# A four-layer graph network on one core: the attention layer rewritten tile by tile, layer norms moved to ScalarE

## The reference

```python
Xq = (H @ W_lin.T).reshape(bt, n, h, dh);  Xv = (H @ W_val.T).reshape(bt, n, h, dh)
e = einsum('behd,hd->beh', leaky_relu(Xq[:, src] + Xq[:, dst], 0.2), a)
e = e + log(A0[src, dst] + 1e-8)[None, :, None]
attn = softmax of e over the edges that share a src
Y = segment_sum(attn[..., None] * Xv[:, dst], src);  return Y.reshape(bt, n, d) @ W_out.T
```

## Time and profile before

| what | us |
|---|---|
| median of three runs | 1168.74 |
| profiled execution | 1168.33 |
| its span (first to last instruction) | 1166.5 |
| TensorE busy | 975.3 (84%) |
| VectorE busy | 743.4 (64%) |
| ScalarE busy | 535.5 (46%) |
| GpSimd busy | 158.7 (14%) |

### The profile page before, as it was taken

The page is one execution under the profiler, slowest core; times in us unless marked ns, Lnnn a source line. Parts: engine busy times, 40 slices in busy tenths (PEclk is TensorE's granted clock), DMA queues, the critical chain, the costliest instruction groups (busy, mean ns, idle before and its releaser), DMA issues.

```text
span 1166.5 us, 15574 instructions
## 1 busy us (share of the span) xinstructions
PE 975.3 (84%) x4413; PEld 666.3 (57%) x4413; DVE 743.4 (64%) x2552; ACT 535.5 (46%) x1387; POOL 158.7 (14%) x390
## 2 busy tenths in 40 slices
PE   4788867878667775995996799989999999999995
PEld 3555545555555654753774788868644456654443
DVE  4567676647678873697666688853454455564576
ACT  1455535537245652332343122223596565555556
POOL 0122222203222220000000000000001111120054
PEclk9699967869565555997997899989999999999998
DMA  9000000000000000000000000000000000000013
GB/s 262 10 1 1 1 1 2 1 1 2 1 1 1 1 1 1 1 1 0 0 0 1 0 0 0 0 1 1 1 1 0 1 1 0 1 1 0 1 36 108
DMA packets 14317, 12.86 MB, mean 11 GB/s; under 512 B 896, under 2 KB 11056, under 8 KB 14256
## 3 DMA queue, kind: packets, MB, share of 16 engines
q1 hardware_dynamic: 14018, 11.98, 3.7%
q10 hardware_dynamic: 238, 0.16, 0.0%
HBM read 7.89 MB, written 4.19 MB: 10 GB/s over the span
## 4 chain that ended last, share of the span: by engine, by line
PE 63%; DVE 24%; issue 5%; ACT 5%; POOL 1%; DVEq 1%; DMA 0%; SPq 0%; POOLq 0%; ACTq 0%
PE bank L844 14%; PE bank L868 8%; PE bank L791 3%; PE bank L776 3%; PE bank L735 3%; PE bank L741 2%; PE bank L749 2%; PE bank L470 2%; PE bank L576 2%; PE bank L811 1%; PE bank L463 1%; PE bank L830 1%; PE bank L817 1%; PE bank L822 1%; DVE hid_t L1942 1%
## 5 line engine op out<-in xcount | busy, mean ns | idle before, releaser
L1268 ACT ACTIVATE hid_t<-bank,gate_b 128x512 f32<-128x512 f32 (+1 forms) x252 | 150.8, 631 | 67.9 <-PE bank L868 66.8
L868 PE MATMUL bank<-ms,w_t 128*128 128x512 f32 (+1 forms) x288 | 112.8, 535 | 6.8 <-DVE ms L1960 6.8
L844 PE MATMUL bank<-hid_t,w_t 128*128 128x336 f32 (+1 forms) x296 | 106.5, 507 | 1.2 <-DVE x L1964 1.2
L1361 POOL COPY hid_t<-feat_t 128x1008 f32<-128x1008 f32 (+1 forms) x12 | 27.8, 2320 | 581.1 <-DVE feat_t L1956 581.1
L844 PE MATMUL bank<-feat_t,w_t 128*128 128x512 f32 x208 | 93.1, 603 | 0.0
L868 PEld LDWEIGHTS bank<-ms,w_t 128*128 128x128 f32 x288 | 54.5, 192 | 56.5 <-issue 34.2
L844 PEld LDWEIGHTS bank<-hid_t,w_t 128*128 128x128 f32 x296 | 56.2, 191 | 46.1 <-issue 26.3
L844 PEld LDWEIGHTS bank<-feat_t,w_t 128*128 128x128 f32 x208 | 39.2, 189 | 51.0 <-issue 46.7
L1275 ACT ACTIVATE hid_t<-hid_t 128x512 f32<-128x512 f32 (+1 forms) x72 | 41.8, 581 | 52.2 <-DVE hid_t L1942 27.6
L1115 ACT ACTIVATE hs<-bank,con 128x1 f32<-128x1 f32 x62 | 16.2, 261 | 102.4 <-PE bank L577 102.4
L1942 DVE TENSOR_TENSOR hid_t<-hid_t 128x512 f32<-128x512 f32 (+1 forms) x36 | 42.2, 1173 | 17.0 <-ACT hid_t L1268 16.9
(11 more groups left out here) (434 smaller groups left out, 2292.8 us busy)
## 6 DMA issues: line engine op xcount, KB each, us to landing
out<-x SPq DMA_DIRECT2D x16, 256.0 KB, 2.6
con<-in_constants SPq DMA_DIRECT2D x1, 449.0 KB, 3.3
hid_t<-in_L_gnn_W SPq DMA_DIRECT2D x2, 128.0 KB, 3.7
e_int<-in_L_gnn_src ACTq DMA_DIRECT2D x1, 128.0 KB
l_w<-in_L_gnn_W SPq DMA_DIRECT2D x2, 64.0 KB
wg<-in_L_gnn_Wg SPq DMA_DIRECT2D x2, 64.0 KB
adj_n<-in_adj SPq DMA_DIRECT2D x1, 64.0 KB, 3.7
hid_t<-in_L_gnn_W_lin SPq DMA_DIRECT2D x1, 64.0 KB, 3.4
```

The source lines that it names most:

```text
L844: return mm(bank[4 * u + BANK_OF[g]][:, 0:w], w_t[:, WB_IH + 4 * (it.p - 1) + g, :], lstm_x(n), start=True, stop=(it.k == 0))
L868: mm(bank[4 * u + BANK_OF[g]][:, 0:w], w_t[:, WB_HH + 4 * (it.p - 1) + g, :], lstm_h_of(it.chain)[:, 0:w], start=False, stop=True).then_in ...
L1268: f(dst[:, 0:w], bank[4 * u + BANK_OF[g]][:, 0:w], ACT.Tanh if g == G_G else ACT.Sigmoid, bias=gate_b[:, 4 * (it.p - 1) + g:4 * (it.p - 1) ...
L1361: pool.tensor_copy(turned[:, g * nb * P:g * nb * P + nb * nw * p].rearrange("q (k a n) -> q k a n", k=p, a=nb), feat_t[:, g * nb:(g + 1) * ...
```

## The change

Nothing changes outside layers 1 to 3 but where the final norm keeps its statistics (they move from `xs[0]` to `perm`). In the changed kernel all hardware loops of these layers are written out.

**Norms.** In layers 1 and 2 VectorE no longer writes the normalised x. It adds into x in place, takes statistics (eight batches together in layer 1, four in layer 2) and computes scale and shift; ScalarE writes x in place. ScalarE's write of a tile stands two turns behind.

**Logits.** Each tile of x is transposed on TensorE, evicted, and used as the held operand against W_lin and W_val side by side (256 columns). The two halves of the result are evicted apart: `z_lin` and `z_val` (in `feat_t`, kept for all 16 tiles). Edge columns are gathered from `z_lin`. The logits are a product that holds a 128-column window of `head_strip` (zeros, with the head vector's 4 columns in one place) and streams the activations; the window slides by 4 rows a batch, and 32 batches add up in one bank. The log of the edge weight is brought to a row by two products with ones.

**Softmax** by halves of 32 batches: the first between tiles 9 to 14 of the logits loop, the second between tiles 0 to 6 of the values loop.

**Values.** The dst rows are gathered from `z_val` by holding `dst_st` and streaming 512 columns. Banks 4 and 5 are now single for the sum by src and for W_out.

**Layer 3** waits for each tile of x by itself.

```diff
+            def ln_written(count, t):
+                act.wait_ge(s["ln_scale"], count)
+                for b in range(TB):
+                    d = f(x[:, t * TB + b, :], x[:, t * TB + b, :], ACT.Identity,
+                          scale=ln_rs[:, t, b:b + 1], bias=ln_shift[:, t, b:b + 1])
+                d.then_inc(s["x_ready"], 1)
```

TensorE's order and products:

```diff
+            def layer2():
+                l2_turn(0)
+                for t in range(TILES):
+                    l2_project(t)
+                    if t + 1 < TILES:
+                        l2_turn(t + 1)
+                    if t == 0:
+                        gcn_floor()
+                    if t == 1:
+                        gcn_bias()
+                    if t:
+                        l2_logits(t - 1)
+                    l2_gather(t)
+                soft_turn(0)
+                l2_values(0)
+                l2_logits(TILES - 1)
+                for t in range(TILES):
+                    if t + 1 < TILES:
+                        l2_values(t + 1)
+                    if t:
+                        l2_out(t - 1)
+                    if t == 6:
+                        soft_turn(1)
+                    l2_scatter(t)
+                l2_out(TILES - 1)
...
+            def l2_turn(t):
+                    d = tr(bank[t % 2][:, b * P:(b + 1) * P], x[:, t * TB + b, :], ident)
...
+            def l2_project(t):
+                        d = mm(bank[2 + k][:, b * E:(b + 1) * E], xs[t % 2][:, 2 * k + b, :], w_t[:, WB_LIN:WB_LIN + 2, :],
+                               start=True, stop=True)
...
+            def l2_gather(t):
+                for k, name in enumerate(("l2_z_act", "l2_z_dve")):
+                    pe.wait_ge(s[name], t + 1)
+                    if t:
+                        pe.wait_ge(s["l2_act"], 2 * t + k - 1)
+                    for b in range(2):
+                        d = mm(bank[4 + k][:, b * E:(b + 1) * E], z_lin[t % 2][:, 2 * k + b, :], sum_st[:, :], start=True, stop=True)
...
+            def l2_logits(t):
+                        r = HEADS * (TB * (t % PAIRS) + 2 * k + b)
+                        d = mm(bank[6 + half][:, 0:E], head_strip[:, P - HEADS - r:2 * P - HEADS - r], rhs[:, b * E:(b + 1) * E],
+                               start=(r == 0), stop=(r == P - HEADS))
...
+            def l2_values(t):
+                    mm(bank[2 * (t % 2) + c][:, :], dst_st[:, c * P:(c + 1) * P], z_val[:, t * TB:(t + 1) * TB, :],
+                       start=True, stop=True).then_inc(s["l2v_val"], 1)
...
+            def l2_scatter(t):
+                pe.wait_ge(s["l2v_w"], 2 * (t + 1))
+                if t:
+                    pe.wait_ge(s["l2v_y_sb"], t)
+                        d = mm(bank[4][:, b * P:(b + 1) * P], w[c][:, b, :], src_s[:, c, :], start=(c == 0), stop=(c == EC - 1))
...
+            def l2_out(t):
+                pe.wait_ge(s["l2v_y_sb"], t + 1)
+                if t:
+                    pe.wait_ge(s["l2v_added"], t)
+                    d = mm(bank[5][:, b * P:(b + 1) * P], ms[t % 2][:, b, :], w_t[:, WB_OUT, :], start=True, stop=True)
```

ScalarE's order (`l2_turned` evicts the four transposes as 512 columns, `l2_kept` copies two times 256 columns out of bank 2, `l2_slope` and `l2_y_kept` are 512 columns each):

```diff
+            def layer2():
+                l2_turned(0)
+                for t in range(TILES):
+                    l2_kept(t)
+                    if t + 1 < TILES:
+                        l2_turned(t + 1)
+                    for k in range(2):
+                        l2_slope(t, k)
+                    if t < 4:
+                        l1_written(TILES - 4 + t)
+                    if t == 1:
+                        l1_root(PAIRS - 1)
+                    if t == 10:
+                        soft_exp(0)
+                for t in range(TILES):
+                    if t == 2:
+                        table_for(ACT.Sqrt)
+                    if t > 1:
+                        l2_root(t - 2)
+                    l2_y_kept(t)
+                    if t == 1:
+                        soft_exp(1)
+                    if t > 1:
+                        l2_written(t - 2)
```

VectorE's order (`l2_kept` copies two times 256 columns out of bank 3, `l2_weighted` is two products of 512 columns; the first half's softmax stands at t 9 to 14, the second half's logits, two maximum scans and difference at t 0, its other steps one a tile at t 1 to 6):

```diff
+            def layer2():
+                for t in range(TILES):
+                    l2_kept(t)
+                    if t == 0:
+                        floor_and_row()
+                        l1_stats(PAIRS - 1)
+                    if t == 1:
+                        gcn_bias()
+                    for k in range(2):
+                        l2_leaky(t, k)
+                    if t == 1:
+                        l1_scaled(PAIRS - 1)
...
+                soft_columns(0)
+                l2_weighted(0)
+                for t in range(TILES):
+                    if t + 1 < TILES:
+                        l2_weighted(t + 1)
+                    if t > 1:
+                        l2_scaled(t - 2)
+                    if t:
+                        l2_added(t - 1)
...
+                    if t:
+                        l2_stats(t - 1)
```

Layer 3 on TensorE:

```diff
             def layer3_gcn():
+                        pe.wait_ge(s["x_ready"], CREDIT + 2 * TILES + 2 * j + u + 1)
-                pe.wait_ge(s["x_ready"], CREDIT + 64)
```

More of the change, by code:

```diff
@@ L441, in edges @@
                 tr(py[0][0:1, 0:P], sc[:, 8:9], ident).then_inc(s["edge_adj"], 1)
-            def ahead(turns, early, work):
-                early(0)
-                with pe.Fori(0, turns - 1) as j:
-                    work(j, lambda: early(j + 1))
-                work(turns - 1, lambda: None)
             def ahead_written_out(turns, early, work):
@@ new lines, in gcn_floor, with gcn_bias @@
+            def gcn_floor():
+                pe.wait_ge(s["l1_added"], CREDIT + TILES)
+                mm(bank[6][:, 0:P], bg0[:, :], rowsum_t[:, :], start=True, stop=True).then_inc(s["gcn_floor"], 1)
+                for c in range(EC):
+                    d = mm(bank[7][:, c * P:(c + 1) * P], ones[:, :], diag_log[:, c, :], start=True, stop=True)
+                d.then_inc(s["log_row"], 1)
+            def gcn_bias():
+                pe.wait_ge(s["gcn_floor_sb"], 1)
+                pe.wait_ge(s["log_row_sb"], 1)
+                mm(bank[7][:, E:E + P], floor[:, :], wg1[:, :], start=True, stop=True).then_inc(s["gcn_floor"], 1)
@@ new lines, in layer1 @@
+                fetched(0)
+                fetched(1)
+                for j in range(PAIRS):
+                    for t in (2 * j, 2 * j + 1):
+                        act.wait_ge(s["l1_hid"], t + 1)
+                        f(ht[t % 2][:, :, :], ph[t % 2][:, :], ACT.Relu, bias=v_cols[:, VR_L1B1:VR_L1B1 + 1]).then_inc(s["l1_hid_sb"], 1)
+                    if j > 1:
+                        l1_written(2 * j - 4)
+                    if j + 1 < PAIRS:
+                        fetched(2 * j + 2)
+                        fetched(2 * j + 3)
+                    if j > 1:
+                        l1_written(2 * j - 3)
+                    if j:
+                        l1_root(j - 1)
@@ L1419, in norm_apply, with ln_added @@
-            def norm_apply(u, nb, first, tile):
-                dve.wait_ge(s["ln_std"], tile + 1)
-                link(dve.reciprocal(rs[:, u, 0:nb], rs[:, u, 0:nb]))
-                for b in range(nb):
-                    t = ts(x[:, bass.ds(first + b, 1), :], ys[u][:, b:b + 1, :], mv[:, u, b, 0:1], rs[:, u, b:b + 1],
-                           ALU.subtract, ALU.mult)
-                t.then_inc(s["x_ready"], 1)
-            def norm_scale(u, nb, tile):
-                dve.wait_ge(s["ln_std"], tile + 1)
-                link(dve.reciprocal(rs[:, u, 0:nb], rs[:, u, 0:nb]))
-                stt(shift[:, u, 0:nb], mv[:, u, 0:nb, 0], -1.0, rs[:, u, 0:nb], ALU.mult, ALU.mult).then_inc(s["ln_scale"], 1)
+            def ln_added(t, src, name):
+                tt(x[:, t * TB:(t + 1) * TB, :], x[:, t * TB:(t + 1) * TB, :], src[:, :].rearrange("p (a b) -> p a b", a=TB), ALU.add)\
+                    .then_inc(s[name], 1)
@@ L1517, in edges @@
                 dve.wait_ge(s["edge_adj"], 2)
[L1518 removed]
+                copy(rowsum_t[:, :], py[0][0:1, 0:P])
             def l0_stats(n):
@@ new lines, in l1_stats, with l1_scaled, head_rows @@
+            def l1_stats(j):
+                dve.wait_ge(s["l1_added"], CREDIT + 2 * j + 2)
+                ln_stats(2 * j, 2)
+            def l1_scaled(j):
+                ln_scaled(TILES + j + 1, 2 * j, 2)
+            def head_rows():
+                dve.wait_ge(s["log_done"], 1)
+                link(dve.memset(head_strip, 0.0))
+                link(copy(head_strip[:, P - HEADS:P], head_a[:, :]))
+                for c in range(EC):
+                    link(ts(diag_log[:, c, :], ident, log_a[:, c:c + 1], None, ALU.mult))
@@ new lines, in l2_kept, with l2_leaky @@
+            def l2_kept(t):
+                dve.wait_ge(s["l2_z"], 2 * t + 2)
+                z = bank[3][:, :].rearrange("p (b k d) -> p b k d", b=2, k=2)
+                copy(z_lin[t % 2][:, 2:4, :], z[:, :, 0, :])
+                copy(z_val[:, t * TB + 2:t * TB + 4, :], z[:, :, 1, :]).then_inc(s["l2_z_dve"], 1)
+            def l2_leaky(t, k):
+                dve.wait_ge(s["l2_slope"], 2 * t + k + 1)
```

(2 more changed lines are left out.)

507 lines of the change are left out of this document (234 added, 273 removed).

## The result

The changed kernel takes 1086.8 us (median of four runs, 1086.33 to 1087.05) against 1168.75: a ratio of 0.9298, 95% interval 0.9282 to 0.9314. A second measurement of the changed kernel gave 1088.06 us, so 0.2 us is less than what separates two medians of it.

What follows compares the result with a forecast made beforehand. TensorE was taken as the bound (63% of the last chain), with idle holes and low-clock starts. Gains of 72.2 plus 2.4 us, 74.6, off 1168.33 gave 1093.7; 2 us for missed waits made 1096, range 1087 to 1114.

Steps and rivals of the forecast that it cites:

- Holes and order: Layers 1 to 3: hole between layers 9.8 to 2.6 us, softmax's 19.05 us to 5.8, layer 3 saves 2.4.
- the smaller values turn: Values: turn falls from 7.19 to 4.64 us since norm write, two evictions and smaller tiles' fixed parts leave.
- the price of the values turn: Values: TensorE sets the turn at 4.64 us a tile, against 3.9 us of work on VectorE.
- The margins: Allowances for stalls in logits and values, and 2 us for 0.1 us waits missed in 40 turns.
- the sum of tile 7 ends about 1 us late: Values: TensorE leads by a turn and catches VectorE, slowed by the second softmax half; about 1 us.
- the way to the first sum: Between logits and values: four transposes, two values products and the last logits, 5.8 us, replace softmax's 19.05 us hole.
- the hole: Between layers 1 and 2: TensorE's wait shrinks to 2.6 us, ScalarE's eviction standing behind a root.
- Layer 1: Layer 1: norm writes leaving VectorE, 2 x 1.11 us a turn, bring turns from 7.96 to 7.3 us.
- Rival 4: Layer 1: ScalarE becomes the last engine, turns of 7.96 us again, +5, so 1101 us; chance 0.10.
- Rival 1: Values: single banks 4 and 5 tie the turn to VectorE, 5.6 us a turn, 1115 us; chance 0.12.
- Rival 2: Logits and values: tiles run one after another, +3.8 and +2.6 us a tile, 1199 us; chance 0.03.
- rival 3: Logits: transposes don't keep the clock up, 16 tiles cost 5.64 us more each, 1186 us; chance 0.01.

Runs made afterwards that it cites:

- u_wait_l2: Changed kernel, but attention's first transposes wait until all of layer 1's norms are written (last roots and writes moved ahead); 1097.05 us.
- u_softmax_one: Changed kernel, but the softmax of both halves runs in one piece between the logits and the values; 1100.77 us.
- u_wait_l3: Changed kernel, but layer 3's first products wait for all of layer 2's norms (last roots and writes moved ahead); 1094.17 us.
- u_norm_l2: Changed kernel, but VectorE writes the normalised x of layer 2 again, four batches a tile; 1093.30 us.
- u_norm_l1: Changed kernel, but VectorE writes the normalised x of layer 1 again, two tiles a turn; 1087.17 us.
- out_twice: Changed kernel with the four W_out products of each values tile issued twice, same result; 1100.53 us.
- half_heads: Changed kernel with half of the head products left out of the logits; 1072.81 us.
- fill_turns: u_wait_l2 with its pause filled by 64 transposes whose results nobody uses; 1096.62 us.
- fill_products: u_wait_l2 with its pause filled by 32 products (64 records) whose results nobody uses; 1097.66 us.

## Where the prediction was right, and why it was 9 us too high

**Holes and order: right.** The projection waits for the eviction behind the root, W_out waits for its eviction twice at the end (0.69 each, priced at 0.8), tile 0 and tile 1 of the logits cost 5.05 and 5.85 us (4.6 and 6.3 predicted), layer 3's first turn is free of the low clock. u_wait_l2, u_softmax_one and u_wait_l3 put single parts back and cost about what those parts were said to bring. By the middle these parts are worth 11.5, 15.8 and 7.1 us, each alone (they need not add up); the smaller values turn, about 4.4 against 7.19 in sixteen turns, is the largest, some 45 us, by the two traces and not by an undoing. The prediction gave it to work that leaves VectorE (the norm write, the evictions). u_norm_l2 puts the norm write back and loses 6.8 us in all; the rows above show that the products by W_val, 2.15 us a turn on TensorE, had to leave as well. The prediction's sum of TensorE's products has them gone, its reason does not name them. No run puts them back.

**The failed step: the price of the values turn.** "TensorE: 1.80 (two of 512) + 0.95 (W_out) + 1.89 (by src) = 4.64 us a tile." Measured 1.72 + 0.89 + 1.78 = 4.39. The mechanism was right here and the size off: these are start-to-start readings of the loops of before, and they hold something of those loops. Before, the sum by src came straight behind VectorE's weighting, so its held operand could not be loaded ahead; in the changed kernel that load starts 0.11 us before the product (660.27 and 660.38, above):

```profile
703.75 1.86 PEld L791 LDWEIGHTS bank<-src_s,ht 128*128 128x128 f32 x16 [0.29 <-DVE ht L1904]
```

There the product starts at 703.75 too and the group takes 1.89 us; with the load ahead it takes 1.78. The products of 512 columns are the same case in smaller: in the earlier trace rows load and product start within 0.02 us of each other (577.16, 577.18), in the changed kernel's values 0.11 apart, and they take 1.80 and 1.72. That these 0.1 us are real and not a fault of reading is seen in layer 1 of the changed kernel, whose second products still wait for the relu:

```profile
476.62 1.86 PEld L715 LDWEIGHTS bank<-l_w,ht 128*128 128x128 f32 x16 [0.75 <-ACT ht L1233]
```

The turn from there is 1.88 + 1.79 + 1.72 + 1.80 = 7.19 us; at 1.72 for products of 512 columns and 1.78 for those of 128 it would be 7.00. So the prices of before were right for groups whose load doesn't run ahead, and together 0.25 us a turn too high where TensorE leads by a turn, which the prediction itself had said of the values. The fourteen turns from 620.57 to 682.36 took 61.8 us against 65.0: 3.2 of the 4.15 us.

**The margins: hardly used.** I added 1 us for stalls in the logits, 1 in the values and 2 us for waits that a walk misses. In the logits TensorE is busy 89.56 us of 89.59; one turn, with the exponential's table load on ScalarE, took 5.91 us instead of 5.62 (587.24 to 593.15), so 0.3 of the first came. In the values the lead over VectorE, one turn, takes up the whole second softmax; "the sum of tile 7 ends about 1 us late" didn't happen. The margins (3.7 unused) and the turn's price (3.2) are 6.9 of the 9.4 us between the sum for the profiled execution (1093.7 and 2) and its time (1086.33); the rest is 0.8 in layer 1, 0.6 in the rest of the logits, 0.6 on the way to the first sum (two transposes too many, and again products of 512 columns at 1.80), 0.4 in the hole, 0.3 in the stage ahead, and crumbs of both signs.

**Layer 1: right number, wrong cause.** 7.3 forecast, 7.19 measured (469.43 to 476.63, and the same through to 519.78). I gave the gain to 2 x 1.11 us that left VectorE; u_norm_l1 put them back and nothing changed. VectorE's turn is 7.08 us with them, not 8.1: two operations on 512 columns back to back take 1.28 us, not 2 x 0.69, and the statistics of eight with their means and variances 2.43 (500.90 to 503.33), not 2.75, so I had also over-priced VectorE. So the right number owes nothing to the moved writes: with them or without, the turn is TensorE's 7.19 us. That it came out right is luck as far as the cause goes. The wait that I named in the earlier trace rows, a relu behind a root behind a variance, is gone in both forms; that it was the cause by itself is likely, not shown. Rival 4 (ScalarE as layer 1's last engine) did not come: the turn is 7.19, and the relu costs TensorE the 0.2 us above, no more.

**The other rivals.** Rival 1 (the single banks tie the values to VectorE) needed turns of 5.6; VectorE has 0.50 us to spare in a turn. u_norm_l2 shows the mechanism real and near: with 1.11 us more on VectorE, turns are 4.56 and the two before tile 6 lose 3.8. Rival 2 (tiles one after another) is refuted by out_twice and half_heads; rival 3 by fill_turns.

**The range.** Its low end stood 9 us under the forecast, and only 5 of them had a reason (table loads and statistics). It held no case "all my high readings and margins are nothing", though this was worth 7 us.

## What to carry to other kernels

Take a price from a turn in which the engine stands as it will stand in the new kernel. For a TensorE that leads by a turn, readings of groups whose load came late are some 0.1 us a group too high (1.89 and 1.80 against 1.78 and 1.72). Add no margin for waits where the walk finds that lead. Before giving a gain to the engine that was relieved, see whether the other one could have gone faster at all: TensorE's 6.72 us of a 7.19 us turn said no. When a stall's chain is ready to read (relu behind root behind variance), first break the chain by order; moving work from one engine to another is a second, separate step with a price of its own, and only an undoing tells which of the two paid. A pause of 5 to 13 us before a dense stage cost here its length and 1.8 to 2 us more of products at the low clock; one of 2.2 us in the LSTM was followed by 1.7 us more in ten profiles and by nothing in four, so two times can differ by that without any edit behind it.

## What the runs showed of the hardware that I had not expected

- Transposes alone raise the clock from 0.50 to 1.00 and hold it, as products do (fill_turns, fill_products): 64 took 8.64 us with the rise, 30 in 3.00 us after it.
- Behind TensorE's wait of 2.50 us in the two filled forms the granted clock over 526 to 530 was 0.66 and 0.58; behind the wait of 1.59 us in the changed kernel it stayed at 1.00. Behind one wait of 2.2 us in the LSTM it fell in ten profiles and stayed at 1.00 in four; the eight products behind it took 4.1 to 4.2 us or 2.53.
- A group of products whose held operand has just been written takes some 0.1 us longer than one whose load runs ahead: 1.89 against 1.78 us for eight of 128 columns (703.75 before, 660.38 after).
- Back to back, two VectorE operations on 512 columns with a bank as operand take 1.28 us, where one alone has 0.69; eight statistics of 128 columns 1.63.
- Code written out instead of looped shows no stall of TensorE: it is busy 89.56 of 89.59 us in the logits.
- In `head_strip` the held window costs TensorE, at each of the offsets used, the 1.73 us that four products of 256 columns take elsewhere.
